# The softmax probabilities of a decoder layer scaled on GpSimd by four products with a per-partition scalar in place of one broadcast product

## The reference, cut to what matters

```python
w = jnp.einsum('bhqd,bhkd->bhqk', q * scale, k * scale)
w = jax.nn.softmax(w.astype(jnp.float32), axis=-1).astype(q.dtype)
out = jnp.einsum('bhqk,bhkd->bhqd', w, v)
```

## Time and profile before

| What | Value |
|---|---|
| Median of 3 runs | 1605.08 us (1603.6 to 1609.28) |
| Time of the profiled execution | 1608.02 us |
| Its span | 1606.1 us |
| TensorE busy | 1419.6 us, 88% |
| VectorE busy | 1335.3 us, 83% |
| ScalarE busy | 976.1 us, 61% |
| GpSimd busy | 966.3 us, 60% |
| First and last start of `scale` | 86.2 us and 1248.0 us |

### The profile page before, as it was taken

The page is one execution under the profiler, slowest core; times in us unless marked ns, Lnnn a source line. Parts: engine busy times, 40 slices in busy tenths (PEclk is TensorE's granted clock), DMA queues, the critical chain, the costliest instruction groups (busy, mean ns, idle before and its releaser), DMA issues.

```text
span 1606.1 us, 37699 instructions
## 1 busy us (share of the span) xinstructions
PE 1419.6 (88%) x10381; PEld 1226.2 (76%) x10381; DVE 1335.3 (83%) x5130; ACT 976.1 (61%) x3763; POOL 966.3 (60%) x1485
## 2 busy tenths in 40 slices
PE   5589999999999999999999999999999399999940
PEld 4378888788888788887788887888888299999940
DVE  4468898989889988889988888988877578888868
ACT  2256666666666666666666666666666156556535
POOL 2445666666666666666666666666654335555568
PEclk6599999999999999999999999999999789999975
DMA  3000000000000000000000000000000378778857
GB/s 86 10 8 8 16 15 16 15 17 16 17 16 15 15 17 17 15 17 14 15 17 18 15 16 15 16 15 18 11 10 12 95 223 246 243 236 250 240 140 205
DMA packets 89610, 96.57 MB, mean 60 GB/s; under 512 B 12137, under 2 KB 75756, under 8 KB 89282
## 3 DMA queue, kind: packets, MB, share of 16 engines
q1 hardware_dynamic: 69714, 71.97, 15.5%
q0 software_dynamic: 8896, 17.20, 3.2%
q10 hardware_dynamic: 10800, 5.06, 1.2%
HBM read 71.88 MB, written 23.35 MB: 59 GB/s over the span
## 4 chain that ended last, share of the span: by engine, by line
DVE 40%; PE 23%; ACT 17%; issue 12%; DMA 3%; POOL 2%; SPq 1%; DVEq 0%; ACTq 0%; POOLq 0%
ACT probs L619 16%; DVE neg_max L764 8%; DVE pT L776 5%; PE ps_u L1416 4%; PE ps_t L1416 3%; DVE k_pick L821 3%; DVE l_hat L868 3%; DVE x1s L851 2%; DMA f_x<-x_rows 2%; DVE turned L807 2%; DVE yT L831 2%; PE ps_s L1262 2%; PE ps_o L1275 1%; PE ps_a L1378 1%; PE ps_t L1295 1%
## 5 line engine op out<-in xcount | busy, mean ns | idle before, releaser
L619 ACT ACTIVATE probs<-ps_s,neg_max 128x128 f32<-128x128 f32 x1024 | 362.6, 366 | 387.7 <-DVE neg_max L764 387.7
L505 POOL TENSOR_TENSOR probs_n<-probs,inv_sum 128x512 f32<-128x512 f32 x256 | 265.1, 1036 | 140.3 <-DVE inv_sum L770 138.4
L1262 PEld LDWEIGHTS ps_s<-kvT,u_sb 128*128 128x128 f32 x2048 | 255.5, 192 | 50.5 <-issue 48.0
L1262 PE MATMUL ps_s<-kvT,u_sb 128*128 128x128 f32 x2048 | 281.1, 280 | 0.0
L1295 PE MATMUL ps_t<-pT,kv_rows 128*128 128x512 f32 x512 | 263.2, 596 | 0.8 <-DVE pT L776 0.8
L1275 PE MATMUL ps_o<-value_w,tT 128*128 128x128 f32 x2048 | 260.6, 275 | 2.5 <-ACT tT L630 2.2
L1275 PEld LDWEIGHTS ps_o<-value_w,tT 128*128 128x128 f32 x2048 | 244.7, 192 | 4.3 <-ACT tT L630 4.3
L567 POOL DMA_INDIRECT y_rows<-wvT,f_id x144 | 144.1, 1001 | 131.9 <-DVE wvT L1176 106.6
L517 POOL DMA_INDIRECT x_rows<-routed,pos_i x128 | 136.8, 1069 | 132.6 <-DVE pos_i L1000 101.3
L619 ACT ACTIVATION_READ_ACCUMULATOR probs<-ps_s,neg_max 128x1 f32 x1024 | 207.6, 203 | 0.0
L1310 PE MATMUL ps_u<-lT_hi,score_hi 128*128 128x256 f32 x512 | 188.4, 368 | 8.6 <-ACT u_sb L660 6.3
(11 more groups left out here) (246 smaller groups left out, 3463.3 us busy)
## 6 DMA issues: line engine op xcount, KB each, us to landing
u_sb<-in_expert_w SPq DMA_DIRECT2D x45, 578.0 KB, 4.8
tT<-in_expert_w SPq DMA_DIRECT2D x27, 578.0 KB
f_x<-x_rows SPq DMA_DIRECT2D x72, 130.0 KB, 2.9
tT<-y_rows SPq DMA_DIRECT2D x32, 256.0 KB, 3.7
x_raw<-in_x SPq DMA_DIRECT2D x64, 64.0 KB, 1.8
c_raw<-in_ctx_in SPq DMA_DIRECT2D x128, 32.0 KB, 2.1
out<-u_sb ACTq DMA_DIRECT2D x16, 256.0 KB, 3.0
y_rows<-wvT,f_id POOLq DMA_INDIRECT x144
```

What stands on the lines that cost most here:

```text
L505: nc.gpsimd.tensor_tensor(probs_n[:, sl], probs[:, sl], inv_sum[:, sl, :].rearrange("p (u o) -> p u o", o=1).to_broadcast([P, UP, P]), ALU ...
L619: last = nc.scalar.activation(probs[:, sl, j], ps_s[sl][:, j * P:(j + 1) * P], ACT.Exp, bias=neg_max[:, sl, j:j + 1], accum_out=sums[:, sl ...
L1262: last = nc.tensor.matmul(ps_s[sl][:, j * P:(j + 1) * P], u_sb[:, c // 2, BT * p + b, h:h + 2].rearrange("p h s -> p (h s)"), kvT[:, c, 1 ...
```

## The change

```diff
@@ scale, on GpSimd
                 n, sl = t * 4 + k, k % 2
                 pool.wait_ge(inv_done, n + 1)
                 pool.wait_ge(pT_ps, count(n - 1))
-                nc.gpsimd.tensor_tensor(
-                    probs_n[:, sl], probs[:, sl],
-                    inv_sum[:, sl, :].rearrange("p (u o) -> p u o", o=1).to_broadcast([P, UP, P]),
-                    ALU.mult).then_inc(p_done, 1)
+                for j in range(UP):
+                    nc.gpsimd.tensor_scalar(probs_n[:, sl, j], probs[:, sl, j], inv_sum[:, sl, j:j + 1], None,
+                                            ALU.mult).then_inc(p_done, 1)
@@ exps, on ScalarE
                 act.wait_ge(max_done, n + 1)
-                act.wait_ge(p_done, count(n - 1))
+                act.wait_ge(p_done, count(UP * (n - 1)))
@@ turn_probs, on TensorE
                 m, ss = t * 4 + (k - 1), (k - 1) % 2
-                pe.wait_ge(p_done, m + 1)
                 pe.wait_ge(pT_done, m)
                 for j in range(UP):
+                    pe.wait_ge(p_done, UP * m + j + 1)
                     last = nc.tensor.transpose(ps_pT[:, j * P:(j + 1) * P], probs_n[:, ss, j], ident[:])
                 last.then_inc(pT_ps, 1)
```

## The result

The changed kernel takes 1637.5 us (1636.9 to 1639.9, four runs) against 1605.3 us (a fourth run joins the three of before): a ratio of 1.0206, 95% interval 1.0191 to 1.0220. It is slower by 2.1%, above the top of my range (1620).

The account below looks back on a forecast made before the run. VectorE's stalls behind GpSimd's product were taken as the bound; the period would fall from 18.43 to 17.95 us, 0.48 us over 62 periods, 30 us off 1608.0, with the median 2.9 us lower: 1575 us, range 1553 to 1620.

Parts of the forecast that it names:

- mechanism that binds the kernel before: VectorE instructions on SBUF data stand until GpSimd's product ends, once in each of four units, together 1.8 us a period.
- rival of TensorE as the bound: L821 and L825 don't stand at all, so the period is 17.70 us and the time 1560 us; chance 0.16.
- step d: Time from one GpSimd product's start to the next's within a unit, taken as 0.30 us.
- the dearest the rows allow: Upper limit of 0.42 us between GpSimd product starts, from a product of two tensors of that size.
- Sizes of the relief: VectorE's stalls behind GpSimd's products shrink: units 0 to 2 give it some 0.6 us a period.
- The hand-over happens at each instruction's end: VectorE gets in between two GpSimd products as each one ends, read from L807 and L947 beside L545 and L547.
- they get 0.17 later, and about 0.3 to 0.5 earlier from the units before: GpSimd's L540 to L547 and `rs_qk`, behind unit 2's product, shift by these us; `rs_qk` ends 0.25 us ahead of L821.
- GpSimd is late: Products 0.42 us apart make `rs_qk` late for L821: 0.12 us a period lost, 1612 us; chance 0.18.
- No hand-over: VectorE gets in only behind a unit's fourth product, each of four stalls grows by 0.17 us: 1647 us; chance 0.07.
- nothing won: Later products stop L853, L979 and L825 as long as L851, L975 and L821 are stopped now: 1605 us; chance 0.07.
- TensorE's waits at nothing: TensorE's three more waits a unit cost nothing; the upper bound was 0.05 us each, 0.6 us a period.
- fixed stretch: TensorE's queue from the start of L1378 to the end of unit 3's `score`, taken as unchanged at 14.19 us.

Follow-up runs that it names:

- four_tensor_products: Changed kernel with each unit's four products as two-tensor products, the inverse sum broadcast over the columns: 1596.2 us, 0.9942 of the kernel before.
- scalar_in_unit_2_alone: Changed kernel with the one broadcast product back in units 0, 1 and 3, four scalar products in unit 2 only: 1729.6 us, 1.051 of the kernel before.
- broadcast_in_unit_2: Changed kernel with the one broadcast product back in unit 2, four scalar products in units 0, 1 and 3: 1606.2 us, 0.979 of the kernel before.

## Why the prediction was wrong, point by point

- *The mechanism that binds the kernel before* was right: VectorE stands behind GpSimd's product at four places, on the chain. Without the product the period is 17.63 us; my rival of TensorE as the bound said 17.70.
- *The step d* is the term that was mis-sized: 0.59 us against 0.30, and above 0.42, which I called "the dearest the rows allow". The bound was an argument (one tensor can't cost more than two) and not a row. Nothing in the trace of before showed a GpSimd tensor_scalar. The sum had 0.17 us more for the four products of a unit; they take 1.35 us more.
- *Sizes of the relief*: 0.93 us in the front stretch alone where I had some 0.5. L820 and L974 end behind the first piece, as I had argued, but the form too lets them pass, which I had not. For two-tensor products the hand-over shows in four_tensor_products and not in the changed kernel, where L806 stood through three products. "The hand-over happens at each instruction's end" was read from one period and is no rule. What decides between the two is open, and no run here tests it.
- *The step that failed in kind*: "they get 0.17 later, and about 0.3 to 0.5 earlier from the units before". I let the relief of units 0 to 2 reach `rs_qk` whole, as if GpSimd's queue before unit 2 stayed loose. The longer product of unit 1 uses up its idle time (1.73 us down to 0.43), so the second stretch takes most of unit 2's 1.35 us (1.23 where it stands alone) and a little of unit 1's, 1.42 in all. Counted from L821, `rs_qk` ends 0.49 us later (18.66 in place of 18.17), with 0.25 of slack.
- *The rival "GpSimd is late"* (0.18) was the right one, though L820 shows no wait for `rs_qk`: it starts 0.34 us behind it, as L806 had held VectorE up. By its own price it would have been far too high: at d = 0.59 its 37 us for each 0.1 beyond 0.40 give about 1675 us, because it let only 0.2 us of relief come from units 0 to 2 and had `rs_qk` and L821's stalls add up; in the changed kernel L820 hardly stands (284 ns). Where both do add up, in scalar_in_unit_2_alone, the period is 19.71.
- *No hand-over* and *nothing won* did not happen as such. *TensorE's waits at nothing*: right (19.05 against 19.00 with fewer of them).
- *The fixed stretch* from L1378 to the scores of unit 3, 14.19 us, was right, but the rest, from the maximum to L1377, grew from 4.04 to 4.77 us in place of falling to 3.73. The chain of the changed kernel in order of time:

```profile
740.77 0.33 PE ps_a L1377
...
754.07 0.91 PE ps_s L1261 x8
754.97 0.02 issue
755.00 0.04 DVE neg_max L763
...
756.11 1.92 DVE turned L806 x2
...
759.77 0.33 PE ps_a L1377
```

754.97 - 740.77 = 14.20 us for the stretch, and 759.77 - 755.00 = 4.77 for the rest, 1.92 of it at L806.

## What to carry to other kernels

An operation whose form the trace does not show has no upper bound from a neighbour of another form: measure it alone, or let the range reach to twice the neighbour. An instruction that has begun and stands behind another engine is booked as busy, and the chain goes over it; ask which engine it ends behind, and whether moving it moves the period at all, before taking it for the cause. When a helper engine gets longer work, sum its whole queue between two hand-overs with the bound engine; slack is a property of such a stretch, and here the same edit gained 0.8% in unit 0 and 1.4% in unit 3 (one run each) and 2.2% in both, and lost 5.1% in unit 2, inside the stretch. And look whether an edit that was to test a theory met the case it was made for: the pauses in GpSimd never met L807.

## What the runs showed of the hardware

- GpSimd's tensor_scalar over fp32 costs 288 ns and 2.5 ns a column (608 ns at 128, 1567 ns at 512), a two-tensor product with one operand broadcast 188 ns and 1.66 ns (405 ns at 128, 1036 at 512): the form with fewer inputs is the slower one. A constant scalar saves 64 ns.
- A VectorE tensor_scalar on SBUF data stands until the end of a two-tensor GpSimd instruction (785 ns, ending 0.03 us behind it). It passes during a one-tensor one over 512 columns: 52 of 53 L819 end 0.71 us behind its start and 0.86 us ahead of its end (318 ns within 1567; 220 ns with no product at all).
- It also stands if it began first: L873 in broadcast_in_unit_2 starts 0.2 us ahead of the broadcast product and ends 0.09 us behind it, 1327 ns on average against 339 with no product.
- A VectorE tensor_tensor stood through three GpSimd two-tensor products in a row, 1.33 us; in four_tensor_products VectorE's tensor_scalars mostly got in between such products (410 to 489 ns on average), and beside one-tensor products L807 took 226 ns.
